# Order of TensorE's passes in the attention slots: the transposed scores' masks ahead of three own passes

## The reference

```python
U = min(L, int(FACTOR * math.log(L)))            # 31
scores = jnp.einsum('bhqd,bhkd->bhqk', Q, K) / math.sqrt(D)
thresh = jax.lax.top_k(scores, U)[0][..., -1:]
scores = jnp.where(scores < thresh, -jnp.inf, scores)
attn = jax.nn.softmax(scores, axis=-1)
context = jnp.einsum('bhqk,bhkd->bhqd', attn, V)
...
x = _layernorm(x + attention(x))
h = silu(x @ wg.T) * (x @ wu.T)
x = _layernorm(x + h @ wd.T)
```

## Time and profile before

| | |
|---|---|
| median of 3 runs | 3479.99 us (3476.94 to 3483.20) |
| profiled execution | 3479.86 us |
| span of its trace | 3478.0 us |
| mean granted clock of TensorE | 0.897 of full speed |
| busy: TensorE, VectorE, GpSimd, ScalarE | 83%, 78%, 68%, 67% |

### The profile page before, as it was taken

The page is one execution under the profiler, slowest core; times in us unless marked ns, Lnnn a source line. Parts: engine busy times, 40 slices in busy tenths (PEclk is TensorE's granted clock), DMA queues, the critical chain, the costliest instruction groups (busy, mean ns, idle before and its releaser), DMA issues.

```text
span 3478.0 us, 83180 instructions
## 1 busy us (share of the span) xinstructions
PE 2872.5 (83%) x21439; PEld 1516.8 (44%) x21439; DVE 2716.7 (78%) x13407; ACT 2336.1 (67%) x5894; POOL 2372.2 (68%) x1549
## 2 busy tenths in 40 slices
PE   5889999697889888866998997988969887787886
PEld 2344545344444444433544453444535444343454
DVE  5888888788878877777887887887878877777861
ACT  3777777585767676655776776766757765576662
POOL 2777778576777766654777786776757765575782
PEclk6899999898999988887999998998979998899886
DMA  2101011110101111011010111101011110110000
GB/s 81 41 20 42 23 40 30 32 26 18 43 23 34 24 34 31 19 32 22 21 44 23 33 26 37 33 25 37 23 32 26 33 33 18 32 26 24 22 14 7
DMA packets 91073, 102.85 MB, mean 30 GB/s; under 512 B 34417, under 2 KB 52850, under 8 KB 90482
## 3 DMA queue, kind: packets, MB, share of 16 engines
q1 hardware_dynamic: 88448, 93.73, 11.2%
q10 hardware_dynamic: 2034, 2.76, 0.2%
HBM read 20.86 MB, written 8.39 MB: 8 GB/s over the span
## 4 chain that ended last, share of the span: by engine, by line
PE 42%; DVE 24%; issue 17%; ACT 9%; DVEq 5%; POOL 2%; SPq 1%; ACTq 1%; DMA 0%; POOLq 0%
DVE cand L855 7%; PE Y_ps L593 6%; PE bench L657 5%; PE bench L663 5%; PE Y_ps L590 4%; PE ctxT_ps L621 4%; PE ST_ps L607 4%; ACT junk L447 4%; PE ST_ps L604 3%; PE Y_ps L591 3%; DVE S L841 3%; DVEq L935 3%; ACT above L455 3%; DVE gtop L916 2%; PE bench L650 2%
## 5 line engine op out<-in xcount | busy, mean ns | idle before, releaser
L1073 POOL TENSOR_SCALAR mask<-S,thr,mb 128x512 bf16<-128x512 f32 x1024 | 2112.1, 2075 | 44.0 <-POOL mb L1067 34.9
L447 ACT ACTIVATE junk<-S,nt 128x512 bf16<-128x512 f32 x1024 | 733.7, 716 | 563.7 <-DVE S L841 549.4
L855 DVE MAX8 cand<-Y_ps 128x8 f32<-128x128 f32 x4096 | 1074.2, 283 | 0.4
L841 DVE TENSOR_SCALAR_CACHE_REDUCE S<-S_ps 128x512 f32<-128x512 f32 x1024 | 702.7, 686 | 275.5 <-PE S_ps L580 216.7
L590 PE MATMUL Y_ps<-ones_b,nbig 128*128 128x512 bf16 x1024 | 421.6, 412 | 521.4 <-DVE cand L855 330.3
L463 ACT ACTIVATE PT<-ST_ps 128x512 f32<-128x512 f32 x1024 | 595.9, 582 | 234.2 <-PE ST_ps L607 233.3
L455 ACT ACTIVATE above<-S,nt 128x512 bf16<-128x512 f32 x1024 | 726.4, 709 | 0.2 <-DVE nt L848 0.2
L1067 POOL TENSOR_SCALAR mb<-rmax 128x8 f32<-128x8 f32 x128 | 31.1, 243 | 894.8 <-DVEq L938 894.8
L580 PE MATMUL S_ps<-KS,QS 64*128 64x512 f32 x1024 | 540.3, 528 | 2.0 <-DMA KS<-Klo 1.4
L593 PE MATMUL Y_ps<-KS,QS 64*128 64x512 f32 x1024 | 539.9, 527 | 0.0
L604 PE MATMUL ST_ps<-QS,KS 64*128 64x512 f32 x1024 | 439.7, 429 | 29.0 <-ACT PT L463 27.2
(11 more groups left out here) (119 smaller groups left out, 4005.4 us busy)
## 6 DMA issues: line engine op xcount, KB each, us to landing
QS<-Qhi SPq DMA_DIRECT2D x512, 32.0 KB, 2.0
KS<-Khi SPq DMA_DIRECT2D x512, 32.0 KB, 2.0
KS<-Klo SPq DMA_DIRECT2D x512, 32.0 KB, 2.0
QS<-Qlo SPq DMA_DIRECT2D x512, 32.0 KB, 2.0
xTs<-in_xT SPq DMA_DIRECT2D x17, 512.0 KB, 3.7
xs<-in_x SPq DMA_DIRECT2D x16, 512.0 KB, 3.9
out<-xs SPq DMA_DIRECT2D x16, 512.0 KB, 2.9
hT<-in_wgT ACTq DMA_DIRECT2D x1, 768.0 KB
```

Source lines behind the costliest of these rows:

```text
L447: nc.scalar.activation(junk[:, :], S[:, score_place(j)[0], :], ACT.Sign, bias=nt0[:, hb, col:col + 1], accum_out=s0[:, j % 8:j % 8 + 1]).t ...
L841: nc.vector.tensor_scalar(S[:, at, :], S_ps[n % 2][:, :], 1.0, None, ALU.mult, op1=ALU.max, accum_out=rmax[:, n % RING:n % RING + 1]).then ...
L855: mx = nc.vector.max(cand[:, j % CANDS, i, :], Y_ps[j % 2][:, i * BW:(i + 1) * BW])
L1073: nc.gpsimd.tensor_scalar(mask[:, h % MASKS, t, :], S[:, score_place(j)[0], :], thr[:, r:r + 1], mb[:, r:r + 1], ALU.is_lt, op1=ALU.add).t ...
```

## The change

The transposed scores' waits and their four mask passes move into a function of their own, `hide_turned`. The two bf16 passes of the masked scores, with their waits, become `hide`. Both are called at the start of a slot, `hide` first. `below` and `turned` keep their places and do only the own pass. The masks now open the accumulation in `ST_ps` (`start=(t == 0)`) and the own pass closes it (`stop=True`) and signals `st_done`. The order in a slot becomes: two bf16 passes, four masks, masked scores' own pass, scores, transposed scores' own pass, values, bench. No instruction is added or removed.

```diff
-            def below(T, n, first):
+            def hide(T, n, first):
                 j = (n - BELOW) % TILES
-                (r, rows), q = stacks(j // NT), j % NT * P
                 Y = Y_ps[j % 2]
                 pe.wait_ge(cnt1_done, T - BELOW + 1)
                 if not (first and n < BELOW + 2):
                     pe.wait_ge(blocks_done, T - BELOW - 1)
                 nc.tensor.matmul(Y[:, :], nbig[:, :], ones_b[:, :], start=True, stop=False)
                 nc.tensor.matmul(Y[:, :], nbig[:, :], above[:, j % 4, :], start=False, stop=False)
+            def below(T, n, first):
+                j = (n - BELOW) % TILES
+                (r, rows), q = stacks(j // NT), j % NT * P
-                nc.tensor.matmul(Y[:, :], QS[rows, r, q:q + P], KS[rows, r, :], start=False, stop=True,
+                nc.tensor.matmul(Y_ps[j % 2][:, :], QS[rows, r, q:q + P], KS[rows, r, :], start=False, stop=True,
                                  tile_position=(rows.start, 0)).then_inc(below_done, 1)
+            def hide_turned(T, n, first):
+                j = (n - TURNED) % TILES
+                h, kt = j // NT, j % NT
+                if kt == 0:
+                    pe.wait_ge(mask_done, T - TURNED + NT)
+                if not (first and n == TURNED):
+                    pe.wait_ge(exp_done, T - TURNED)
+                for t in range(NT):
+                    nc.tensor.matmul(ST_ps[:, t * P:(t + 1) * P], mask[:, h % MASKS, t, kt * P:(kt + 1) * P], nbig[:, :],
+                                     start=(t == 0), stop=False)
             def turned(T, n, first):
...
-                if kt == 0:
-                    pe.wait_ge(mask_done, T - TURNED + NT)
-                if not (first and n == TURNED):
-                    pe.wait_ge(exp_done, T - TURNED)
-                nc.tensor.matmul(ST_ps[:, :], KS[rows, r, kt * P:(kt + 1) * P], QS[rows, r, :], start=True, stop=False,
-                                 tile_position=(rows.start, 0))
-                for t in range(NT):
-                    mm = nc.tensor.matmul(ST_ps[:, t * P:(t + 1) * P], mask[:, h % MASKS, t, kt * P:(kt + 1) * P], nbig[:, :],
-                                          start=False, stop=(t == NT - 1))
-                mm.then_inc(st_done, 1)
+                nc.tensor.matmul(ST_ps[:, :], KS[rows, r, kt * P:(kt + 1) * P], QS[rows, r, :], start=False, stop=True,
+                                 tile_position=(rows.start, 0)).then_inc(st_done, 1)
...
             def slots(b, first, rest):
                 for n in range(TILES):
                     T = b * TILES + n
+                    if due(BELOW, n, first, rest):
+                        hide(T, n, first)
+                    if due(TURNED, n, first, rest):
+                        hide_turned(T, n, first)
                     if due(BELOW, n, first, rest):
                         below(T, n, first)
```

## The result

The changed kernel takes 3525.68 us (median of 4 runs, 3523.21 to 3529.84) against 3478.47 us of the kernel before, measured beside it: 1.0137 times as long, 95% interval 1.0119 to 1.0155. That is 47 us slower where 10 were forecast, and above the top of the range (3516). The profiled execution spans 3527.8 us at a mean clock of 0.894.

The account below looks back on a forecast made before the run. The prediction took the chain passing between three nearly tied engines, TensorE, VectorE and ScalarE, as the bound. Terms -23.3 + 15.1 + 15.7 - 1 + 4 = +10.5 us gave 3490 us, with an 8-in-10 range of 3465 to 3516.

Parts of the forecast that it names:

- Step 1: TensorE's pass order: one change of mode fewer in slots with values, 0.11 us in 212 slots, -23.3 us.
- Step 2: Scores and masked scores start 0.24 us later; 63 chain exits into VectorE's score copy, +15.1 us.
- step 5: Paths close to the chain: 157 other waits for scores grow by 0.24; a tenth taken, +4 us.
- Step 3: TensorE's wait for the exponential stands earlier, behind `above`: 436 stalls, 95 us, of which +15.7 us counted.
- The sign that was set: At TensorE's mask passes: a wait above 150 us would show the exponential-wait term wrong in size.
- scores are late everywhere: Rival: all 220 VectorE waits for scores grow, ScalarE's for `S` too; +46 us, 3526 us, chance 0.07.
- The rival in which the saving wins: Slots with values on the chain: late scores are absorbed and the saved mode change wins; 3462 us, chance 0.22.
- a clock below 0.90: TensorE's mean clock: a lower one, from pauses now inside a slot, would be an unpriced cost.

Follow-up runs that it names:

- e7: Kernel before with the four masks ahead of the transposed scores' own pass, all else as before: 3673.0 us, ratio 1.0571.
- e1: Kernel before with only TensorE's wait for the exponential moved right behind the above pass, in all slots: 3509.86 us, ratio 1.0094.
- e3: Changed kernel with the changed order in even slots alone, odd slots in the order of before: 3480.56 us, ratio 1.0017.
- e4: Kernel before with the values ahead of the masks, no wait or scores moved: 3477.04 us, ratio 1.0005.
- e5: Changed kernel with the order of before in slots 2, 3, 9, 24, 25, 37, 38 and 41: 3484.29 us, ratio 1.0025.
- e10: Changed order only in even slots without 2, 24 and 38, the rest in the order of before: 3477.95 us, ratio 1.0015.
- e12: Changed order in even slots without 2, 24, 38, plus ScalarE's exponential ahead of its context copy: 3467.76 us, ratio 0.9977 to the kernel before.
- e14: Changed order in all slots but 2, 3, 24, 37, 38, plus ScalarE's exponential ahead of its context copy: 3482.14 us, ratio 1.0010.
- e15: Kernel before with values ahead of the masks and ScalarE's exponential ahead of its context copy: 3479.52 us, ratio 1.0006.
- e8: Kernel before with an added pass of zeros behind the above pass, ahead of own passes and scores: 3541.89 us, ratio 1.0197.
- e9: Kernel before with the same added pass of zeros behind the four masks: 3525.69 us, ratio 1.0122.
- e6: Kernel before with the early wait for the exponential only in eight slots with late exponentials: 3506.68 us, ratio 1.0085.

## Why the prediction was wrong, step by step

*Step 1, the saved change of mode (-23.3).* The transitions were right to 0.01 us. The Trainium skill's rule that a change of mode drains and another tile doesn't ("TensorEngine Tiling (Array Packing)", Key Properties) fits own pass to values, 0.32, as one drain. It is no proof of it: from one own pass to the next, with no change of mode between, takes 0.34, and in `e7` own pass to values takes 0.43. So 0.11 us is not the price of a change as such, but of these neighbours. The Trainium skill's rule on weight loads ("TensorE: Matmul & The Clock Gate", The mechanism), by which the first mask's load would show behind `above`, did not hold here: that step is 0.21, as long as the one from `ones_b` to `above`. But of the 23.3 us little came to the end, and this is the second step that failed. What the runs leave for it is the rest of the sum: 47 = 33 (wait, `e1`) + 16 to 26 (lateness) - saving, so 2 to 12 us, and nothing if lateness costs 5. Of `e3`, `e4`, `e5`, `e10`, `e12`, `e14` and `e15` none was faster than the same kernel without the saving, though each has some cost beside it. A piece of the chain can be shortened only until another path becomes the longest, and I read the loss so, since VectorE and ScalarE are nearly tied with TensorE. No run tests that by itself.

*Step 2 and step 5, lateness (+19).* Right in size by the ratios of `e8` and `e9`, 16 to 26 us, and too high if their difference in clock is chance (5 us). VectorE's wait for the scores grew by 34 us, within the 15 to 50 forecast, but the early wait without any lateness of the order (`e1`) makes 18 of them.

*Step 3, the wait for the exponential (+15.7).* This is the step that failed most plainly, and the better shown of the two. The stall itself was forecast well: 95 us in 436 slots, against 87 us in 297 read from the trace after; the slots with long ones were visible too. Its share was not. I took only what lay on the chain of before, 9.8 us of long and 5.9 us of short stalls. Measured, the long ones cost 30 us (`e6`) and the short ones 3 (`e1` less `e6`, which the intervals hardly tell from nothing). A stall that is longer than what its slot has in hand puts the slot on the chain: in the slot shown the scores came 1.05 us later, 0.67 of it by the stall, and had 0.68 in hand. In `e6` 51 stalls with 36 us stood on the chain, not 29 with 9.8. And I capped a stall at 0.45 for passing through, but the scores and all else queued behind the waiting pass bear all of it. The prediction named what was queued there and did not weigh it. The scores are not the whole of it either. In the trace of before, exponential end + 0.06 against `above` + 0.31 gives the stalls of `e1`, 76 us in 130 slots; less the time for which the scores lay ready in each, they sum to only some 11 us. The rest must have come through other work behind the wait, and which is open. The sign that was set, a wait of the masks above 150 us, is passed by the row of the weight load (265.0), but not by the starts (87).

*Sum.* -23.3 + 19.1 + 15.7 - 1 = +10.5 became about -2 to -12 + 16 to 26 + 33 = +47, if the parts add up, which `e10` puts in doubt. The measured time is that of the rival "scores are late everywhere" (3526), but by luck and not by its mechanism, which wanted 53 us from lateness; measured are 16 to 26 (at most 42 by the intervals). The rival in which the saving wins is refuted: the kernel is slower, and no version with the saving was faster than the same kernel without it.

*The clock.* The prediction said that a clock below 0.90 would be a cost that no term has. The four runs of the change have 0.892 to 0.894; the profiled execution of before has 0.897, and the medians of before in the later groups are 0.900 or 0.901. By its two levels, half speed and full, that is 0.6 to 1.4% of the span more at the low one. Half of it, taken for the 42% of the span in which TensorE holds the chain, is an estimate of 4 to 10 us, and no run tests it. In `e1` (0.897 to 0.900) the clock is nearly that of before, so the 33 us of the wait are not the clock's.

## What to carry to other kernels

When a wait is moved ahead of other work on an in-order engine, compare its lateness slot by slot with the slack of everything queued behind it, and not only with the chain of before: that chain tells what a shortening is worth at most, and what a lengthening costs at least. Look for the few slots in which the producer has odd work ahead: here the waits of eight slots in 64 cost 30 us, and hundreds of short ones 3. And a late producer may be cheaper to mend at its own engine than to cover on another: two calls exchanged on ScalarE gave 0.29%, and no order of TensorE's passes that was tried gave anything.

## What the runs showed of the hardware that was not expected

First, two 64-row matmuls on different halves of the rows start within 0.01 us of each other and take no longer than one (1705.11 and 1705.12 in `e7`, 0.43 to the next start as for the single pass). Such a pass that stands between 128-row ones takes 0.43 us to the next start, where two behind one another take 0.34 and 0.32.

Second, TensorE time has no single price. The mean granted clock of three runs (span and clock of the profiled execution; 1.2 and 2.4 GHz are its two levels):

With the masks between (`e7`), with the pass of zeros ahead (`e8`), and with it behind (`e9`):

```profile
core 0: 3666.3 us, clock 0.876
```

```profile
core 0: 3535.3 us, clock 0.923
```

```profile
core 0: 3530.4 us, clock 0.923
```

Some 246 us of longer steps between passes cost 197 us, at a clock that fell from 0.897 to 0.876. Some 220 us of added matmul columns cost 42 to 68 us (49 to 66 by the medians), at a clock that rose to 0.923. From 0.897 to 0.923 the share of the span at the low level falls from 21% to 15%. That the clock makes the whole difference was not tested; that it was higher with the added passes (0.919 to 0.932 in all eight runs) and lower with the longer steps (0.869 to 0.881 in four) is what the three versions show.
